# A four-layer transformer kernel: the second layer's eight experts, from all rows through every expert to rows sorted by expert

## The reference, cut to what matters

```
logits = xf @ Wr                              # 8 experts
probs = softmax(logits); topk_p, topk_i = top_k(probs, 2); topk_p /= sum(topk_p)
gate[token, topk_i] = topk_p                  # 2 of 8 are not zero
shared = new_gelu(xf @ Wfc_s + bfc_s) @ Wproj_s + bproj_s
routed = sum over e of (new_gelu(xf @ Wfc[e] + bfc[e]) @ Wproj[e] + bproj[e]) * gate[:, e]
x = x + modulation * (shared + routed)        # 128 -> 512 -> 128 in each expert
```

## Time and profile before

| | us |
|---|---|
| median of 3 runs | 4036.28 (4019.64 to 4040.5) |
| profiled execution: its own time | 4006.55 |
| its span, first to last instruction | 4004.7 |
| second layer's feed-forward part in it | 1463.8 to 2064.8 |
| of that, norm / combine / experts | 43.4 / 30.1 / 527.5 |

### The profile page before, as it was taken

How to read it: one execution, slowest core, us unless ns; L and a number is a source line. 1 busy time by engine, 2 the same in 40 slices (tenths; PEclk the granted TensorE clock), 3 DMA queues, 4 the chain that set the end, 5 groups by cost and what they waited for, 6 DMA issues and landing times. The chain is left out here.

```text
span 4004.7 us, 71964 instructions
## 1 busy us (share of the span) xinstructions
PE 3023.2 (75%) x20738; PEld 1870.4 (47%) x20738; DVE 2388.8 (60%) x5571; ACT 1445.8 (36%) x3108; POOL 915.0 (23%) x976
## 2 busy tenths in 40 slices
PE   5787433158888876999978986777779984459799
PEld 4555433146655653444435554555634461145344
DVE  5665841178887854333347765555555579984555
ACT  2555100026555534333326661444432221113321
POOL 2222118633333320000002222223200034430000
PEclk6899766569999988999989996888889985569899
DMA  3332313434333310000001111222100000000000
GB/s 70 41 42 42 109 38 55 63 63 53 44 48 45 41 49 3 1 0 0 0 8 27 23 19 21 34 33 35 39 2 0 0 3 0 0 5 22 4 0 21
DMA packets 125781, 111.13 MB, mean 28 GB/s; under 512 B 25177, under 2 KB 115938, under 8 KB 121570
## 3 DMA queue, kind: packets, MB, share of 16 engines
q1 hardware_dynamic: 103474, 93.91, 13.7%
q0 software_dynamic: 20912, 12.58, 2.1%
q10 hardware_dynamic: 1152, 1.61, 0.1%
HBM read 35.28 MB, written 13.86 MB: 12 GB/s over the span
## 5 line engine op out<-in xcount | busy, mean ns | idle before, releaser
L1408 DVE TENSOR_TENSOR f1eHS<-f1eSG,bank 128x512 f32<-128x512 f32 x256 | 175.9, 687 | 319.8 <-PE bank L1336 234.5
L1314 PE MATMUL bank<-f1NT,f1W 128*128 (+1 forms) x576 | 296.4, 596 | 15.8 <-DMA f1eSELB<-in_sel 15.3
L549 ACT ACTIVATE a1PR<-bank 128x384 f32<-128x384 f32 x512 | 242.8, 493 | 149.0 <-PE bank L607 145.1
L1336 PE MATMUL bank<-f1eHS,f1W 128*128 128x512 f32 x576 | 293.8, 592 | 0.0
L784 DVE TENSOR_REDUCE a1NM<-bank 128x3 f32<-128x384 f32 x512 | 262.8, 549 | 28.4 <-PE bank L589 25.7
L1367 ACT ACTIVATE f1eSG<-bank,f1eFB 128x512 f32<-128x512 f32 x256 | 175.8, 687 | 283.5 <-PE bank L1314 161.7
L784 DVE TENSOR_REDUCE a4NM<-bank 128x3 f32<-128x384 f32 x256 | 132.9, 551 | 136.8 <-PE bank L589 134.7
L787 DVE TENSOR_REDUCE a2NMQ<-bank 128x2 f32<-128x512 f32 x256 | 168.1, 685 | 60.6 <-PE bank L593 60.4
L953 PE MATMUL bank<-ONES 128*128 128x256 bf16 x960 | 172.0, 287 | 24.2 <-DMA f3nWR<-in_wr 4.6
L784 DVE TENSOR_REDUCE a0NM<-bank 128x3 f32<-128x384 f32 x256 | 133.8, 551 | 94.7 <-PE bank L589 93.5
L549 ACT ACTIVATE a4PR<-bank 128x384 f32<-128x384 f32 x256 | 122.3, 489 | 187.0 <-PE bank L607 186.4
(11 more groups left out here) (633 smaller groups left out, 8613.5 us busy)
## 6 DMA issues: line engine op xcount, KB each, us to landing
a1QH<-a1SPL SPq DMA_DIRECT2D x96, 64.0 KB
a1KH<-a1SPL SPq DMA_DIRECT2D x96, 64.0 KB
a1QH<-a1QH SPq DMA_DIRECT2D x96, 64.0 KB
a1KH<-a1KH SPq DMA_DIRECT2D x96, 64.0 KB
f1W<-in_w SPq DMA_DIRECT2D x2, 2304.0 KB, 10.8
sums<-rZT SPq DMA_DIRECT2D x2, 2112.0 KB
sW<-in_w SPq DMA_DIRECT2D x1, 4096.0 KB, 12.5
xLD<-sums SPq DMA_DIRECT2D x16, 256.0 KB, 5.7
```

The lines of the kernel that those rows point to most:

```text
L549: nc.scalar.activation(PR[:, h % 8, :], bank[2 + h % 2][:, 0:NC], ACT.Exp, scale=SCALE)\
L1314: pe.matmul(bank[q][:, :], W1[:, m * P:(m + 1) * P], x, start=True, stop=True).then_inc(g_ready.sem, 1)
L1336: mm = pe.matmul(bank[6 + j][:, :], W2[:, m, :], HS[:, m % 4, :], start=(m == 0), stop=(m == NCH - 1 and CBF is None))
L1408: v.tensor_tensor(HS[:, m % 4, :], a, bank[4 + (j * NBC + kth[m]) % 2][:, :], ALU.mult).then_inc(hs_ready.sem, 1)
```

## The change

`ffn` for this layer is replaced by `routed_ffn`, with these blocks.

1. The same norm (into `c.HT` instead of a tile of its own). It fetches the shared expert's up weights and all down weights ahead; the routed up weights stay in HBM.
2. A routing block in place of `combine_phase`. The gates are made by the same steps. Then each token gets a place for each of its two experts in a list of 10240 rows: 40 tiles of 256 rows (`TILES = 2 * 4096 / 256 + 8`), each tile for one expert, every expert's rows padded to a multiple of 256. A row in HBM (`rows_by_slot`) has 130 floats, the input, the token's number and its gate. The tile's expert is in `EXPERT`. SyncE writes zeros over the rows and over two accumulators (`routed`).
3. `experts_phase` with the four shared chunks alone. Beside it GpSimd writes the 2 x 32 x 128 rows to their places by 64 indirect transfers (no accumulation), and waits for all of them.
4. A loop over the 40 tiles, written out. SyncE loads the expert's number into a register, fetches that expert's up weights (256 KB, 4 buffers) and the tile's rows (130 KB, 8 buffers). TensorE turns the rows (2 transposes), multiplies up (4 products of 256 columns), loads the expert's number into a register and multiplies down (8 products of 128 columns, tokens back on the partitions). ScalarE loads the number too, for the bias. VectorE multiplies by the gate, and GpSimd adds 2 x 128 rows to the two sums. The end is that of `sparse_ffn`.

```diff
@@ experts_phase, GpSimd
+            if cfg.get("rows"):
+                rows, slot, place, rows_out = cfg["rows"]
+                for n in range(NT_TILES):
+                    for k in range(2):
+                        nc.gpsimd.indirect_dma_start(place[:, :], bass.IndirectOffsetOnAxis(slot[:, k, n:n + 1], 0), rows[:, k, n, :], None,
+                                                     bounds_check=place.shape[0] - 1, oob_is_err=True).then_inc(rows_out, 16)
+                pool.wait_ge(rows_out, 16 * 2 * NT_TILES)
+def routed_ffn(c, cfg):
...
+            @block.sync
+            def _(sp):
+                sp.dma_start(TAB[:, :], c.ins["tiles8"]).then_inc(tab_in.sem, 16)
+                after(sp, zeroed, 0, 1)
+                rows = XS.rearrange("(p n) d -> p (n d)", p=P)
+                for k in range(5):
+                    sp.dma_start(rows[:, 2080 * k:2080 * k + 2080], ZB[:, 0:2080]).then_inc(zero_out.sem, 16)
+                for a in range(2):
+                    rows = ACC[a].rearrange("(p n) d -> p (n d)", p=P)
+                    for k in range(2):
+                        sp.dma_start(rows[:, 2112 * k:2112 * k + 2112], ZB[:, :]).then_inc(sums_zero, 16)
+                after(sp, zero_out, 0, 16 * 5)
...
+        experts_phase(c, dict(cfg, name="f1", NCH=4, sel=[None] * 4, glu=False, hbias="hb1s", rows=(XTM, SLOT, XS, rows_out)),
+                      NT, W1, None, W2[:, 32:36, :], None, CBF, w_in, 2)
...
+            @block.sync
+            def _(sp):
+                sp.dma_start(FB[:, :], c.ins["hb1r"]).then_inc(b_in.sem, 16)
+                for j in range(TILES):
+                    expert = sp.value_load(EXPERT[0:1, j:j + 1], min_val=0, max_val=E - 1)
+                    if j >= 4:
+                        after(sp, up_done, 0, 2 * j - 6)
+                    sp.dma_start(WT[:, j % 4, :], WALL[:, bass.ds(expert * 512, 512)]).then_inc(weights_in[j % 4].sem, 16)
+                    if j >= RING:
+                        after(sp, y_copied, 0, j - RING + 1)
+                    sp.dma_start(XG[:, j % RING, :, :], XS[j * TILE:(j + 1) * TILE, :].rearrange("(p s) d -> p s d", p=P))\
+                        .then_inc(rows_in[j % RING].sem, 16)
...
+            @block.gpsimd
+            def _(pool):
+                pool.wait_ge(sums_zero, 16 * 4)
+                for j in range(TILES):
+                    after(pool, y_copied, 0, j + 1)
+                    for a in range(2):
+                        if j:
+                            pool.wait_ge(added[a], ADDED0 + 16 * j)
+                        nc.gpsimd.indirect_dma_start(ACC[a][:, :], bass.IndirectOffsetOnAxis(ID2[:, j % 4, a:a + 1], 0), Y[:, j % 4, a, :], None,
+                                                     bounds_check=DUMMY + NTOK - 1, oob_is_err=True, compute_op=ALU.add).then_inc(added[a], 16)
+
+            @block.tensor
+            def _(pe):
+                for t in range(TILES + 2):
+                    j = t - 1
+                    if 0 <= j < TILES:
+                        after(pe, weights_in[j % 4], 0, 16 * (j // 4 + 1))
+                        after(pe, turned_copied, 0, j + 1)
+                        for m in range(4):
...
+                            mm = pe.matmul(bank[2 + j % 2 * 2 + m // 2][:, m % 2 * TILE:(m % 2 + 1) * TILE],
+                                           WT[:, j % 4, m * P:(m + 1) * P], XT2[:, j % 2, :], start=True, stop=True)
...
+                    j = t
...
+                        for s in range(2):
+                            mm = pe.transpose(bank[j % 2][:, s * P:(s + 1) * P], XG[:, j % RING, s, 0:D], c.ID)
...
+                    j = t - 2
+                    if 0 <= j:
+                        expert = pe.value_load(EXPERT[0:1, j:j + 1], min_val=0, max_val=E - 1)
+                        after(pe, h_done, 0, 2 * j + 2)
...
+                        for s in range(2):
+                            for m in range(4):
+                                w2 = W2[:, bass.ds(expert * 4 + m, 1), :].rearrange("p m d -> p (m d)")
+                                mm = pe.matmul(bank[6 + j % 2][:, s * P:(s + 1) * P], HS[:, j % 2, m, s * P:(s + 1) * P], w2,
+                                               start=(m == 0), stop=(m == 3))
...
@@ build
-        ffn(c, dict(xnorm, name="f1", layer=1, nmod=3, gmod=5, wr="wr1", E=8, renorm=True, NCH=36,
-                    sel=[m // 4 for m in range(32)] + [None] * 4, glu=False, fn=ACT.Gelu_apprx_tanh,
-                    w1="w1_1", w2="w2_1", selector="sel1", hbias="hb1", ybias="yb1", ebias="eb1"))
+        routed_ffn(c, dict(xnorm, name="f1", layer=1, nmod=3, gmod=5, wr="wr1", E=8, fn=ACT.Gelu_apprx_tanh,
+                           w1="w1_1", w2="w2_1", ybias="yb1", ebias="eb1"))
```

More of the change, by code:

```diff
@@ L2037, in layout @@
     i["wr0"], i["rbias"] = f(x["L0_ffn_gate_w"].T), f(np.broadcast_to(x["L0_ffn_gate_bias"], (P, 64)))
-    i["w1_1"] = f(np.concatenate([up(x["L1_ffn_Wfc"]), x["L1_ffn_Wfc_s"]], 1))
+    i["w1_1"], i["w1_1s"] = up(x["L1_ffn_Wfc"]), f(x["L1_ffn_Wfc_s"])
     i["w2_1"] = f(np.concatenate([down(x["L1_ffn_Wproj"]), down(x["L1_ffn_Wproj_s"])], 1))
-    i["hb1"] = f(np.concatenate([chunks(x["L1_ffn_bfc"]), chunks(x["L1_ffn_bfc_s"])], 1))
+    i["hb1r"], i["hb1s"] = chunks(x["L1_ffn_bfc"]), chunks(x["L1_ffn_bfc_s"])
+    p = np.arange(P, dtype=np.float32)[:, None]
+    i["tiles8"] = f(np.concatenate([P + p * NT_TILES + np.arange(NT_TILES)[None, :], np.broadcast_to(np.arange(40)[None, :], (P, 40)), p], 1).astype(np.float32))
     i["wr1"], i["yb1"], i["eb1"] = f(x["L1_ffn_Wr"]), col(x["L1_ffn_bproj_s"]), f(x["L1_ffn_bproj"])
@@ L2045, in layout @@
     i["hb4"], i["yb4"] = chunks(x["L3_attn_fc_b"]), col(x["L3_attn_proj_b"])
-    i["sel1"], i["sel2"], i["sel3"] = selector(8, 128, 8), selector(4, 128, 4), selector(8, 176, 11)
+    i["sel2"], i["sel3"] = selector(4, 128, 4), selector(8, 176, 11)
     return i
```

229 lines of the change are left out of this document (added).

## The result

The changed kernel takes 3794.2 us (median of 4 runs, 3786.59 to 3795.19), the kernel before, on the same chip, 4027.96 us (median of 4, 4007.57 to 4040.5). The ratio is 0.942, with a 95% interval of 0.9375 to 0.9465. The forecast was 3804 us.

A forecast was written before the change was run, and what follows sets the result against it. TensorE's streamed columns were taken to bound the experts' stage; afterwards GpSimd's chain of adds. Terms summed to 368.6 us against 601.0, 232.4 less, so 4036.3 became 3804 us; own range 3783 to 3830, 8 in 10 within 3775 to 3880.

The forecast's parts named there:

- routing: Block replacing the choosing of experts: 42 dependent VectorE steps behind the gates, 25 us (19 to 30) instead of 30.1.
- shared block with the scatter: GpSimd's 64 writes end last, 87 us plus 2 for the last landing: 89 (86 to 123), hiding TensorE's 68.
- filling: Start of the tile loop: first load, then transposes, up and down products at the low clock; 16 us to the first add.
- 39 tiles: Tile loop: GpSimd's two adds with their waits set the period, 4.4 us a tile (4.1 to 5.0), 171.6 us together.
- end: After the last add's landing, the same end as in the first layer: 18.2 us.
- The stretch by the loads: Tile loop: loads beside the adds lengthen the 4.12 us period by 0.3, taken from earlier landings, to 4.4.
- rival A: Tile loop: the loads delay the adds, period 5.0 us, 23 us more, 3828; chance 0.10.
- B: Tile loop: TensorE stops at its register load, 5.35 us a tile, 37 us more, 3841; chance 0.17.
- C: Scatter: a plain write by list costs what an add costs, 121 us instead of 87, 34 more, 3838; chance 0.10.
- D: Tile loop: TensorE stays at 1.2 GHz, 7.3 us a tile, 113 us more, 3917; chance 0.08.
- E: Tile loop: slower than before, period reaching 10.4 us, which needs adds landing in about 9.6 us; chance 0.03.
- The signs named for a right forecast: Two adds each 4.1 to 5.0 us, writes each 1.3 to 1.4, TensorE's loop clock 0.9 or more, waits naming VectorE's copy.

The follow-up runs named there:

- the four traces of this loop: The changed kernel twice, one run with half the scatter writes, one with their wait moved to SyncE; period 4.69 to 4.76 us over the first 30 tiles.
- three sums: The changed kernel with three accumulators in place of two, an add waiting for the third before it: 3765.57 us, ratio 0.9381.
- the one with four loads: The three-accumulator kernel with TensorE's register load done four times a tile instead of once: 3782.52 us in one run.
- the three amounts of load: The changed kernel with weights kept on chip, loaded once, or loaded twice: 130, 386 and 642 KB beside two adds, period 4.35, 4.75 and 5.12 us.

## Why the prediction was right, and which terms were off

**What bounds it before.** TensorE's columns were the price: the experts' five stages take 311.4 us (91.7 + 16.6 + 146.6 + 38.6 + 17.9) instead of 527.5, and TensorE is busy for 234.5 of them (67.44 + 10.47 + 133.10 + 14.61 + 8.92) instead of 520.0. It is no longer what ends last.

**The sum.** Forecast and measured, term by term:

| | forecast | measured |
|---|---|---|
| norm | 43.4 | 43.4 |
| routing | 25 | 23.8 |
| shared block with the scatter | 89 | 91.7 |
| filling | 16 | 16.6 |
| 39 tiles | 171.6 (4.4 each) | 179.9 (4.61 each) |
| second add, landing | 2 + 3.4 | 2.1 + 3.2 |
| end | 18.2 | 17.9 |
| sum | 368.6 | 378.6 |

The saving is 222.4 us in the two traces, 10 less than forecast, and 8.3 of these 10 lie in the period. Here the mechanism was right and a size off: the adds' chain sets the period, and VectorE and TensorE wait behind it as described. The stretch by the loads was taken as 0.3 from the landings of the earlier trace rows; while loads run it is about 0.6 here (4.75 against 4.16), and 0.4 to 0.6 in the four traces of this loop. Those rows had 96 KB of fetches each 3.3 us, and the loop has 386 KB of loads each 4.6 us, three times as much in a us. The forecast had named this factor itself, under rival A, but did not scale the 0.3 by it.

**Two errors met in the scatter's term.** A write costs 1.32 us on average, not 1.36, so that 64 of them take 84 us instead of 87; 2 us were added for the last landing where 7.15 pass, since GpSimd leaves the block late. That cost was not foreseen, and the forecast gave no row for it.

**The median was nearer than the sum, by luck.** The profiled executions differ by 212.0 us, the feed-forward part by 222.4. The rest is in untouched stages: 2.6 us ahead of the part, 7.7 behind it. Most of the latter is the next layer's attention, whose row is this in the changed kernel and, in the second fence, with three sums:

```profile
1899.80:2188.10 288.30, 260.43 (x2401) 158.02 (x2404) 212.11 (x459) 187.72 (x379) 76.94 (x129) 0.96 0.13 22
```

```profile
1875.90:2158.40 282.50, 254.62 (x2405) 156.38 (x2404) 211.96 (x459) 187.90 (x379) 76.97 (x129) 0.98 0.14 23
```

It is the same work at a granted clock of 0.96 and of 0.98 (0.99 and 281.2 us in the kernel before), and TensorE's busy time carries the difference. It does not look like chance alone: all six traces with two sums have 287.7 to 293.1 us here at 0.94 to 0.96, both traces of three sums without added register loads have 282.5 at 0.98, and the one with four loads has 293.7 at 0.95. So by the traces some 7 us of the saving go in a stage that the forecast took as untouched, and of the 24.9 us between the medians of two and three sums some 8 lie there (290.4 against 282.5). Why the clock differs was not tried, and of before there is one trace. On the other side, the runs of before have a median 21.4 us above their profiled execution, those of the change do not. So the medians differ by 233.8, next to the forecast 232.4: the forecast's 3804 was met within 10 us, partly by that spread. The experiment that ran the kernel again, with 11 runs of before beside it, has 224.2 between the medians, 8 less than forecast.

**The rivals.** *A*, that loads delay the adds: its mechanism is there, shown by the three amounts of load, at something over half of its price (4.75 instead of 5.0 while loads run, 4.61 over all). The Trainium skill's rule ("DMA: Bandwidth & Descriptors", Issuing engines are not separate DMA queues) is that transfers interleave on the same engines, whoever issues them; the trace agrees, with loads issued by SyncE and a median landing of GpSimd's adds of 3.6 us beside them and 3.2 behind them. *B*, that TensorE stops at its register load: not in this kernel (0.22 us from transposes to down products); part of it appears when four loads stand in a row. *C*, that a write costs what an add does: no, 0.97 us for most against 1.55. *D*, the low clock: no, 1.00 while loads run. *E*, landings of 9.6 us: the longest is 4.8.

**What would show it.** The signs named for a right forecast came, with two differences: most writes start a little sooner than the 1.3 to 1.4 us named, and TensorE's idle time ahead of the up products (13 us in the fifth stage) is put down to "issue" and not to VectorE's copy. That it waits behind VectorE follows from the program's order and from VectorE's 95.8 us behind the adds.

## What to carry to other kernels

An accumulating transfer that waits for its predecessor's landing is a chain: the landing sets its period, which grows by a part of every load that runs beside it. A third accumulator takes the landing out of the chain and is worth more (28 us of the part here) than taking the weights' loads away (15); with it the loads are free. When a period is estimated from landings in another stage, ask how many bytes a us ran beside them there, and scale the stretch by that. And a busy share near 1 over a stage does not make an engine its bound: look whether it is only getting ahead into free buffers.

## What the hardware showed that was not expected

- A block whose last work on GpSimd is an indirect transfer is left about 5.5 us late, with every engine and all DMA engines idle; 33 us after the last such transfer the same border costs 0.29. The late case was seen at one border, behind 64 writes in a row.
- A write of 128 rows by a list holds GpSimd for 0.97 us in most cases (up to 1.23), a little less than a fetch (1.01 to 1.06) and much less than an accumulating one (1.55).
- A register load from a tile on chip is a record of 0.30 us on TensorE's queue. One was free, and three more added 0.47 us to a tile instead of 0.91.
